# Twelve attention passes on one core: scores computed query by key and transposed after the softmax, against scores computed key by query with row maxima found beforehand

## The chip, the cores and the metric

One core of a Trainium2 chip runs the whole kernel in one launch. The metric is device time in microseconds; the median of three runs counts, and lower is better. PE is TensorE, DVE VectorE, ACT ScalarE, POOL GpSimd; SP issues the loads.

## The reference, cut to what matters

A layer norm, a graph aggregation, a linear attention, and then a block with three chained softmax attentions and an MLP, all on 1250 rows of 512 features. The change concerns the three attentions, each of 8 heads of 64 features: spatial (plain), temporal (causal) and cross, whose queries come from the spatial result and whose keys and values come from the temporal one.

```python
att = softmax(einsum('bthd,bshd->bhts', q, k), axis=-1)      # q scaled by HD ** -0.5
o = einsum('bhts,bshd->bthd', att, v)
spatial_out = _spatial_experts(xn, ...)                      # one expert's weights
temporal_out = _temporal_experts(xt, ...)                    # causal mask, xt + o
fused = _cross_mha(spatial_out, temporal_out, ...)
x = x + fused
```

The result has to be near fp32, so nearly every product is taken in parts: a number is split into a rounded part (`hi`, type fp32r) and the rest (`lo`), and hi x hi, hi x lo and lo x hi are added in PSUM.

## The kernel before, in words

Each engine has its own queue, written out in program order, and they meet by counting semaphores. Attention is 12 passes of two heads each: n = 0 to 3 spatial, 4 to 7 temporal (causal), 8 to 11 cross. The tokens are 10 tiles of 125 rows, two tiles (250) a pair, and a batch is one head of one query pair against one key pair: 50 batches in a full pass, 30 in a causal one, 520 in all.

In a pass PE does, in the order of one list `STEPS`:
- `unit` (L1892): Q and K for both heads, feature by token, in six pieces of 418 columns with 12 matmuls each; ACT writes hi (`unit_hi`, L1124) and DVE lo (`unit_lo`, L1493).
- `values` (L1930): V token by feature, 12 matmuls of 128 columns for each tile, split by ACT (L1163) and DVE (L1549).
- `score` (L1951, L1959, L1961): one query tile against up to 512 keys for the two heads at once, each head in 64 of the array's rows, in three pairs of matmuls; causal pieces add a mask (L1956).
- `turned` (L1976): four transposes of 125x125 of the finished probabilities into PSUM.
- `product` (L1992): four matmuls of 250 columns that add V times the turned probabilities into the one bank `OUT_BANK`.

Between them, DVE takes each score piece out of PSUM scaled, with its row minimum of the negated scores (`shift`, L1516), ACT takes the exponential and its sum over a whole row of up to 1250 keys (`exponent`, L1144), DVE the reciprocal of the sum, one number a row (`recip`, L1529), and POOL multiplies the row by it (`prob`, L940). PE transposes only after POOL. A turned batch is split by ACT (`pt_hi`, L1181) and DVE (`pt_lo`, L1581, which reads PSUM and `pt_hi`). ACT and DVE bring an output out together (L1152, L1539), since the two value parts of a head stand in different halves of the array. Transposes run `AHEAD` = 3 batches ahead of products, in a ring of three banks. The next pass's Q and K stand among the last batches of a pass; passes 0 and 8 have an opening of their own. Before pass 8 the temporal output projection (`project`, L2005) joins in.

POOL splits the weight blocks (`split`, L848 and L850), eight blocks for the folded spatial output projection during pass 1, and the attention outputs in `feat` into planes (`split_plane`, L931 and L933). SP loads 256 KB weight blocks into three slots.

After attention (L2041, L2070) follow the output projection and the MLP, which the change leaves as they are, as it does all before attention.

## Time and profile before

| what | us |
|---|---|
| runs, in order | 2180.33, 2180.38, 2619.19 |
| median | 2180.38 |
| the profiled execution | 2188.32 |
| its span, first to last instruction | 2186.5 |
| mean granted TensorE clock | 0.941 of 2.4 GHz |

The rows below come from the profiled execution. A span starts at its first instruction. Busy time of PE counts overlapping matmuls once, and a matmul's own duration holds its way through the array, so what a matmul costs in a row of like ones is read from start to start. "issue" is time in which an engine waited for nothing that the profile shows.

### The profile page before, as it was taken

To read this page: it belongs to the slowest core of one execution; us is meant where nothing else is said; L and a number is where in the kernel's file an instruction comes from. 1 tells how busy PE (TensorE), PEld (TensorE's weight loads), DVE (VectorE), ACT (ScalarE), POOL (GpSimd) and SP (SyncE) were. 2 spreads that over 40 slices of the span, in tenths; PEclk is the share of its full clock that TensorE was granted. 3 is DMA by queue.
4 is the path that set the end of the run, shared out by engine and by line. 5 is a ranking of instruction groups with operands and counts; after the bars stand their busy time and mean duration, and the time that the engine had idled before them with its cause. 6 is when DMAs were issued, how large, how long until landed. Compare 5 with 4: busy or idle time off the path is not lost.

```text
span 2186.5 us, 35324 instructions
## 1 busy us (share of the span) xinstructions
PE 1885.5 (86%) x11839; PEld 1604.6 (73%) x11839; DVE 1302.4 (60%) x3667; ACT 828.7 (38%) x1490; POOL 602.7 (28%) x575
## 2 busy tenths in 40 slices
PE   1999999866898998989888887888989898876998
PEld 1687577655787886979777776777878786776886
DVE  6576577766676546575645546457676767552332
ACT  0223111022565545565544435246565655320000
POOL 2210011001324315141322213513231315546330
PEclk9999999957999998999989999899999999997999
DMA  3001000023000000020000000000000001002101
GB/s 97 30 6 44 6 25 15 1 104 119 15 1 25 20 30 15 18 92 1 16 1 15 11 6 16 18 6 12 1 16 1 16 1 72 29 28 68 39 29 47
DMA packets 24417, 60.83 MB, mean 28 GB/s; under 512 B 2522, under 2 KB 4790, under 8 KB 23373
## 3 DMA queue, kind: packets, MB, share of 16 engines
q1 hardware_dynamic: 24260, 58.74, 8.0%
q8 instruction: 98, 1.61, 0.3%
q14 instruction: 59, 0.48, 0.1%
HBM read 44.87 MB, written 13.86 MB: 27 GB/s over the span
## 4 chain that ended last, share of the span: by engine, by line
PE 56%; issue 14%; POOL 13%; DVE 10%; ACT 4%; DMA 1%; DVEq 1%; SPq 1%; POOLq 0%; ACTq 0%
PE ps L1892 7%; POOL probs L940 7%; PE ps L1992 7%; PE ps L2041 6%; PE ps L1976 6%; PE ps L1716 5%; PE ps L1930 4%; PE ps L1796 3%; PE ps L2070 3%; PE ps L1828 3%; PE ps L1951 3%; DVE probs L1516 2%; PE ps L1729 1%; DVE pt_lo L1581 1%; ACT pt_hi L1181 1%
## 5 line engine op out<-in xcount | busy, mean ns | idle before, releaser
L940 POOL TENSOR_SCALAR probs<-probs,stats 125x1250 f32<-125x1250 f32 (+4 forms) x240 | 280.8, 1180 | 926.0 <-DVE stats L1529 926.0
L1581 DVE TENSOR_TENSOR pt_lo<-ps,pt_hi 125x500 fp32r<-125x500 f32 x520 | 351.3, 677 | 186.2 <-ACT pt_hi L1181 181.2
L1181 ACT ACTIVATE pt_hi<-ps 125x500 fp32r<-125x500 f32 x520 | 304.8, 588 | 368.0 <-PE ps L1976 363.8
L1976 PE MATMUL ps<-ident,probs 125*125 125x125 f32 x2080 | 332.3, 286 | 87.3 <-POOL probs L940 87.3
L1992 PE MATMUL ps<-pt_hi,v_tok 125*128 125x250 f32 x1040 | 319.0, 328 | 55.5 <-DVE feat L1539 55.3
L1976 PEld LDWEIGHTS ps<-ident,probs 125*125 125x125 f32 x2080 | 285.7, 198 | 103.0 <-POOL probs L940 96.3
L1516 DVE TENSOR_SCALAR_CACHE_REDUCE probs<-ps 125x416 f32<-125x416 f32 (+5 forms) x624 | 340.6, 585 | 16.2 <-PE ps L1961 15.3
L1992 PEld LDWEIGHTS ps<-pt_hi,v_tok 125*128 125x128 f32 x1040 | 204.0, 196 | 139.4 <-DVE pt_lo L1581 77.5
L1144 ACT ACTIVATE probs<-probs,stats 125x1250 f32<-125x1250 f32 (+4 forms) x240 | 286.1, 1193 | 15.1 <-DVE stats L1521 15.1
L1992 PE MATMUL ps<-pt_lo,v_tok 125*128 125x250 f32 x1040 | 274.9, 286 | 0.0
L1992 PEld LDWEIGHTS ps<-pt_lo,v_tok 125*128 125x128 f32 x1040 | 205.5, 198 | 0.4
L1375 DVE TENSOR_SCALAR onehot<-iota_h,win_key,key_t 125x320 f16 x453 | 169.9, 375 | 0.5 <-issue 0.3
L1374 DVE TENSOR_SCALAR onehot<-iota_h,low_t 125x125 f16 x453 | 126.8, 280 | 61.8 <-PE ps L1828 31.8
L1951 PE MATMUL ps<-k_hi,q_hi 64*125 64x416 f32 (+5 forms) x624 | 146.9, 467 | 8.7 <-DVE k_lo L1493 5.8
L1930 PE MATMUL ps<-w_hi,xa_hi 128*125 128x128 f32 x480 | 131.3, 274 | 0.0
L1930 PE MATMUL ps<-w_lo,xa_hi 128*125 128x128 f32 x480 | 130.9, 273 | 0.0
L1930 PE MATMUL ps<-w_hi,xa_lo 128*125 128x128 f32 x480 | 130.8, 272 | 0.0
L1959 PE MATMUL ps<-k_hi,q_lo 64*125 64x416 f32 (+5 forms) x624 | 118.4, 375 | 0.0
L1961 PE MATMUL ps<-k_lo,q_hi 64*125 64x416 f32 (+5 forms) x624 | 114.7, 363 | 0.0
L1828 PE MATMUL ps<-onehot 125*125 x453 | 86.8, 312 | 17.8 <-DVE onehot L1375 17.3
L1796 PE MATMUL ps<-near_rows,adj 125*125 125x257 f32 (+1 forms) x400 | 94.5, 388 | 2.4 <-issue 2.1
L1951 PEld LDWEIGHTS ps<-k_hi,q_hi 64*125 64x125 f32 x624 | 59.8, 188 | 49.4 <-DVE k_lo L1493 7.6
(341 smaller groups left out, 3494.8 us busy)
## 6 DMA issues: line engine op xcount, KB each, us to landing
w_raw<-in_w_mlp SPq DMA_DIRECT2D x32, 256.0 KB, 2.6
w_raw<-in_w_gps SPq DMA_DIRECT2D x16, 256.0 KB, 2.6
w_raw<-in_w_tp SPq DMA_DIRECT2D x16, 256.0 KB, 2.6
w_raw<-in_w_sp SPq DMA_DIRECT2D x12, 256.0 KB, 5.4
w_raw<-in_w_cr SPq DMA_DIRECT2D x12, 256.0 KB, 2.6
d_xt<-xb_hi SPq DMA_DIRECT2D x1, 2508.0 KB, 9.3
d_xt<-xb_lo SPq DMA_DIRECT2D x1, 2508.0 KB, 14.9
xa_hi<-d_xt SPq DMA_DIRECT2D x1, 2508.0 KB, 9.6
```

The source lines that it names most:

```text
L940: pool.tensor_scalar(p, p, stats[:, slot, 7:8], 1.0, ALU.mult, ALU.mult).then_inc(s_prob, 1)
L1144: act.activation(p, p, ACT.Exp, scale=-1.0, bias=st[:, least:least + 1], accum_out=st[:, 4:5]).then_inc(s_exp, 1)
L1181: act.activation(pt_hi[:, (BASE_B[n] + m) % PT, :], ps[0:TOK, ring_bank(ring_of(n, m)), 0:4 * TOK], ACT.Copy)\
L1375: ins = dve.tensor_scalar(row[:, ET:ET + DH], iota_h[0:ET, :], win_key[0:ET, bass.ds(w, 1)], key, ALU.add, ALU.is_equal)
L1516: dve.tensor_scalar(probs[:, slot + h, first:first + w], ps[0:TOK, bank + h, 0:w], -SCALE, None, ALU.mult, ALU.min, accum_out=stats[:, slo ...
L1581: dve.tensor_tensor(pt_lo[:, slot, :], ps[0:TOK, ring_bank(ring_of(n, m)), 0:4 * TOK], f32(pt_hi[:, slot, :]), ALU.subtract).then_inc(s_pt ...
L1796: ins = pe.matmul(ps[0:TOK, bank + h, 0:257 - h], adj[t // 4][:, x, cols], near_rows[:, x, h, 0:257 - h], start=(x == 0), stop=(x == NT - 1))
L1892: ins = pe.matmul(ps[:, x % 4, 0:NP], w[:, k % 3, 128 * c:128 * c + 128], src[:, c, NP * p:NP * p + NP], start=(c == 0 and y == 0), stop=( ...
L1930: ins = pe.matmul(ps[0:TOK, ring_bank(r), 128 * t:128 * t + 128], x[:, c, (t0 + t) * TOK:(t0 + t + 1) * TOK], w[:, k % 3, 128 * c:128 * c ...
L1951: pe.matmul(ps[0:TOK, bank + h, 0:w], q_hi[r, tile], k_hi[r, first:first + w], start=True, stop=False)
L1976: ins = pe.transpose(ps[0:TOK, ring_bank(r), x * TOK:(x + 1) * TOK], probs[:, slot, kt * TOK:(kt + 1) * TOK], ident[0:TOK, 0:TOK])
L1992: ins = pe.matmul(ps[:, OUT_BANK, 0:2 * TOK], v_tok[:, kt, y % 2, :], part[:, slot, 2 * TOK * x:2 * TOK * (x + 1)], start=(kt == 0 and par ...
```

## The change

The attention passes are written anew; what comes before and after stays.

- Scores are computed key by query: 125 keys on the partitions, 250 queries in the columns. The exponential then has the layout that the product with V needs, and the transposes of the probabilities go away, as does POOL's scaling.
- A row maximum can't be taken over partitions, so it is found beforehand: `maximum` multiplies the rounded parts alone, query by key, for both heads at once (L2126), DVE reduces the two banks (L1654), joins the pieces (L1662), PE turns the column of maxima into a row (L2142), and ACT writes it negated into a 65th row of the queries' second operand (L1235), against a row of ones in the keys' operand. The score matmul so subtracts it by itself.
- K and Q are stored twice: `k_both`, `q_both`, `k_rest`, `q_row` hold hi and lo of a head in the two halves of 128 partitions. A score is two matmuls for a key tile: hi keys on 64 rows and again on 64 (against hi and lo queries), then the rest of the keys with the maximum (L2170, L2174). The causal mask is added to the score (L2172).
- ACT takes the exponential of a step's 125x500 scores twice from the same bank: once rounded into `p_hi` and once in full into `p_raw`. DVE subtracts, both inputs in SBUF, into `p_lo`.
- The product has V beside 64 columns of ones (`v_ones`), so the sum of the probabilities stands in the lower half of the output bank, and adds V's rest (`v_rest`) in a matmul of its own: six matmuls for a step. Two banks take turns.
- The end of a unit (one head of one query pair): DVE takes the reciprocal of 64x250 sums, and multiplies (L1686, L1688).
- V is computed feature by token in three pieces, written to `feat` by ACT, and turned by PE (L2152).
- A planner (`plan_steps`) puts the linear pieces K, V, Q, the maxima M, the rows R, the turned values T and the fold F as side tasks between the steps of the pass before, by due dates and costs, and `pool_plan` puts the weight splits 12 steps ahead. Scores run `LEAD` = 2 steps ahead of products; scores and probabilities have rings of three.
- The last plane before the join is split by ACT and DVE, not by POOL.

```diff
+            def exponent(g):
+                act.wait_ge(s_score, g + 1)
+                if g >= PR:
+                    act.wait_ge(s_p_lo, g - PR + 1)
+                if g >= PR:
+                    act.wait_ge(s_pv, g - PR + 1)
+                act.activation(p_hi[:, g % PR, :], ps[0:TOK, g % 3, 0:4 * TOK], ACT.Exp, scale=SCALE).then_inc(s_p_hi, 1)
+                act.activation(p_raw[:, g % PR, :], ps[0:TOK, g % 3, 0:4 * TOK], ACT.Exp, scale=SCALE).then_inc(s_exp, 1)
...
+            def maximum(n, i, y, j):
...
+                dve.wait_ge(s_max, MAX_NO["M", n, i, y, j])
+                dve.tensor_reduce(part[:, y, :, j], ps[0:TOK, 5:7, 0:w], AX.X, ALU.max).then_inc(s_max_part, 1)
...
+            def p_low(g):
+                dve.wait_ge(s_p_hi, g + 1)
+                dve.wait_ge(s_exp, g + 1)
+                if g >= PR:
+                    dve.wait_ge(s_pv, g - PR + 1)
+                dve.tensor_tensor(p_lo[:, g % PR, :], p_raw[:, g % PR, :], f32(p_hi[:, g % PR, :]), ALU.subtract).then_inc(s_p_lo, 1)
+
+            def unit_out(g):
+                n, i, h, _ = STEP[g]
+                u = unit_of(g)
+                dve.wait_ge(s_pv, g + 1)
+                dve.reciprocal(share[:, u % 2, :], ps[64:128, 3 + u % 2, 0:2 * TOK]).then_inc(s_share, 1)
+                dve.wait_ge(s_share, u + 1)
+                dve.tensor_tensor(feat[HALF[h], n % 4, 2 * TOK * i:2 * TOK * (i + 1)], ps[0:64, 3 + u % 2, 0:2 * TOK], share[:, u % 2, :],
+                                  ALU.mult).then_inc(s_o, 1)
...
+                for g in range(first, end):
+                    for what, *at in SIDE[g]:
+                        if what == "M":
+                            maximum(*at)
+                    if g > first and ends(g - 1):
+                        unit_out(g - 1)
+                    if g + LEAD < end:
+                        p_low(g + LEAD)
...
-            def prob(n, u, h):
...
-                pool.tensor_scalar(p, p, stats[:, slot, 7:8], 1.0, ALU.mult, ALU.mult).then_inc(s_prob, 1)
...
+                for x in range(2):
+                    tile = slice((2 * b + x) * TOK, (2 * b + x + 1) * TOK)
+                    to = ps[0:TOK, g % 3, 2 * TOK * x:2 * TOK * (x + 1)]
+                    pe.matmul(to, k_both[h][:, n % 2, tile], q_both[h][:, ring(n, i), :], start=True, stop=False)
...
+                    ins = pe.matmul(to, k_rest[h][rest, n % 2, tile], q_row[h][rest, ring(n, i), :], start=False, stop=True)
...
-                    ins = pe.transpose(ps[0:TOK, ring_bank(r), x * TOK:(x + 1) * TOK], probs[:, slot, kt * TOK:(kt + 1) * TOK],
...
+                    pe.matmul(ps[:, bank, 0:2 * TOK], v_ones[:, kt, h, :], p_hi[:, g % PR, cols], start=(b == 0 and x == 0), stop=False)
+                    pe.matmul(ps[:, bank, 0:2 * TOK], v_ones[:, kt, h, :], p_lo[:, g % PR, cols], start=False, stop=last)
+                    ins = pe.matmul(ps[0:64, bank, 0:2 * TOK], v_rest[:, kt, h, :], p_hi[:, g % PR, cols], start=False, stop=last,
+                                    skip_group_check=True)
```

DVE's queue in a cross pass of the kernel before, around the end of one head's query pair (`pt_lo` is a batch's rest, `probs,stats` a score piece with its minimum, `feat` the output):

```order
L1516 TENSOR_SCALAR probs,stats<-ps 125x416 x2
L1521 TENSOR_REDUCE stats<-stats 125x2
L1529 RECIPROCAL stats<-stats 125x2
L1581 TENSOR_TENSOR pt_lo<-ps,pt_hi 125x500
L1539 SCALAR_TENSOR_TENSOR feat<-ps,vecs,o_half 64x250
L1581 TENSOR_TENSOR pt_lo<-ps,pt_hi 125x500
L1529 RECIPROCAL stats<-stats 125x1
L1581 TENSOR_TENSOR pt_lo<-ps,pt_hi 125x500
L1529 RECIPROCAL stats<-stats 125x1
```

Two rests stand within two instructions of the output, and every reciprocal is one or two numbers wide.

DVE's queue in a cross pass of the changed kernel, at the end of a unit (`p_lo` is a step's rest, `max_part` a maximum's reduction over two banks, `share` the reciprocal):

```order
L1654 TENSOR_REDUCE max_part<-ps 125x2
L1686 RECIPROCAL share<-ps 64x250
L1688 TENSOR_TENSOR feat<-ps,share 64x250
L1679 TENSOR_TENSOR p_lo<-p_raw,p_hi 125x500
L1654 TENSOR_REDUCE max_part<-ps 125x2
L1679 TENSOR_TENSOR p_lo<-p_raw,p_hi 125x500
L1654 TENSOR_REDUCE max_part<-ps 125x2
L1679 TENSOR_TENSOR p_lo<-p_raw,p_hi 125x500
L1654 TENSOR_REDUCE max_part<-ps 125x2
L1662 TENSOR_REDUCE max_col<-max_part 125x2x2
L1679 TENSOR_TENSOR p_lo<-p_raw,p_hi 125x500 x2
```

A reciprocal of one or two numbers a row has become one of 250, with the multiplication behind it, and it stands in front of the next step's rest and the next maximum.

PE's queue in a cross pass before, a batch's transposes, a score piece and a product:

```order
L1976 MATMUL ps<-ident,probs 125x125 x4
L1951 MATMUL ps<-k_hi,q_hi 125x418 x2
L1959 MATMUL ps<-k_hi,q_lo 125x418 x2
L1961 MATMUL ps<-k_lo,q_hi 125x418 x2
L1992 MATMUL ps<-pt_hi,v_tok 128x250
L1992 MATMUL ps<-pt_lo,v_tok 128x250
L1992 MATMUL ps<-pt_hi,v_tok 128x250
L1992 MATMUL ps<-pt_lo,v_tok 128x250
```

Each group works on another batch: the transposes three batches ahead of the product.

PE's queue in a cross pass after, a step's scores, a maximum's pair and a product:

```order
L2170 MATMUL ps<-q_both_a,k_both_a 125x250
L2174 MATMUL ps<-q_row_a,k_rest_a 125x250
L2170 MATMUL ps<-q_both_a,k_both_a 125x250
L2174 MATMUL ps<-q_row_a,k_rest_a 125x250
L2126 MATMUL ps<-k_both_a,q_both_a 125x418
L2126 MATMUL ps<-k_both_b,q_both_b 125x418
L2188 MATMUL ps<-p_hi,v_ones 128x250
L2189 MATMUL ps<-p_lo,v_ones 128x250
L2190 MATMUL ps<-p_hi,v_rest 64x250
L2188 MATMUL ps<-p_hi,v_ones 128x250
L2189 MATMUL ps<-p_lo,v_ones 128x250
L2190 MATMUL ps<-p_hi,v_rest 64x250
```

The four transposes and two of three score pairs are gone; four score matmuls of 250 columns and two more product matmuls have come.

## Rows read from the trace of the kernel before

**Rows 1.** The page, part 1: busy time of the engines.
```profile
PE 1885.5 (86%) x11839; PEld 1604.6 (73%) x11839; DVE 1302.4 (60%) x3667; ACT 828.7 (38%) x1490; POOL 602.7 (28%) x575
```

**Rows 2.** The line that writes outputs: duration ns min/median/max, first and last start us.
```profile
L1539 DVE SCALAR_TENSOR_TENSOR feat<-ps,sp_vecs,o_half x40: 457/476/487, 569.7 to 1040.5; 64x250 f32<-64x250 f32 x40
L1539 DVE SCALAR_TENSOR_TENSOR feat<-ps,tp_vecs,o_half x40: 459/477/489, 1051.7 to 1385.6; 64x250 f32<-64x250 f32 x40
L1539 DVE SCALAR_TENSOR_TENSOR feat<-ps,vecs,o_half x40: 459/475/485, 1471.2 to 1882.0; 64x250 f32<-64x250 f32 x40
```

**Rows 3.** Busy time by stretch: causal, full, all attention.
```profile
core 0: us, PE busy (x) PEld busy (x) DVE busy (x) ACT busy (x) POOL busy (x), PEclk, DMA share, GB/s
1100.00:1200.00 100.00, 82.22 (x599) 72.08 (x597) 53.55 (x151) 47.24 (x101) 24.58 (x29) 0.91 0.03 9
...
1500.00:1600.00 100.00, 93.76 (x711) 81.78 (x709) 69.90 (x201) 58.49 (x103) 25.64 (x21) 1.00 0.02 7
...
515.00:1885.00 1370.00, 1210.30 (x8725) 1054.87 (x8726) 845.68 (x2335) 701.17 (x1276) 436.63 (x417) 0.95 0.06 21
```

**Rows 4.** Waits in attention: us in total, times, longest us.
```profile
PE ps L1976 <- POOL probs L940: 87.3, 39, 5.1
...
PE ps L1992 <- DVE feat L1539: 55.3, 72, 1.6
```

**Rows 5.** PE's timeline in pass 0: start us, us, engine, line, operation.
```profile
641.64 0.38 PE L1992 MATMUL ps<-pt_hi,v_tok 125*128 125x250 f32 x1
641.87 0.28 PE L1992 MATMUL ps<-pt_lo,v_tok 125*128 125x250 f32 x1
641.98 0.28 PE L1992 MATMUL ps<-pt_hi,v_tok 125*128 125x250 f32 x1
...
642.21 0.60 PE L1976 MATMUL ps<-ident,probs 125*125 125x125 f32 x4
642.74 0.45 PE L1951 MATMUL ps<-k_hi,q_hi 64*125 64x418 f32 x2
643.03 0.35 PE L1959 MATMUL ps<-k_hi,q_lo 64*125 64x418 f32 x2
643.22 0.36 PE L1961 MATMUL ps<-k_lo,q_hi 64*125 64x418 f32 x2
643.51 0.38 PE L1992 MATMUL ps<-pt_hi,v_tok 125*128 125x250 f32 x1
```

**Rows 6.** The chain that ended last: start us, us, what.
```profile
515.36 16.30 PE ps L1892 x72
...
624.40 2.30 PE ps L1892 x12
...
785.46 5.39 PE ps L1930 x48
```

**Rows 7.** ACT's groups: operation, shapes, count, busy us, mean ns.
```profile
L1181 ACT ACTIVATE pt_hi<-ps 125x500 fp32r<-125x500 f32 x520 | 304.8, 588 | 368.0 <-PE ps L1976 363.8
...
L1124 ACT ACTIVATE k_hi<-ps,vecs 128x418 fp32r<-128x418 f32 x12 | 7.3, 611 | 21.5 <-PE ps L1892 21.5
```

**Rows 8.** DVE's timeline in pass 0.
```profile
641.38 0.68 DVE L1581 TENSOR_TENSOR pt_lo<-ps,pt_hi 125x500 fp32r<-125x500 f32 x1
641.98 0.58 DVE L1516 TENSOR_SCALAR_CACHE_REDUCE probs<-ps 125x416 f32<-125x416 f32 x1
```

**Rows 9.** Timeline ahead of attention: POOL and DVE, both inputs in SBUF.
```profile
496.43 1.57 POOL L850 TENSOR_TENSOR w_lo<-w_raw,w_hi 128x512 fp32r<-128x512 f32 x1
496.80 1.73 DVE L1293 TENSOR_TENSOR xb_lo<-norm_tmp,xb_hi 128x500 fp32r<-128x500 f32 x1
...
504.13 0.67 DVE L1293 TENSOR_TENSOR xb_lo<-norm_tmp,xb_hi 128x500 fp32r<-128x500 f32 x1
```

**Rows 10.** DVE's groups by form, whole kernel.
```profile
L1539 DVE SCALAR_TENSOR_TENSOR feat<-ps,vecs,o_half 64x250 f32<-64x250 f32 x40 | 18.9, 473 | 7.7 <-ACT o_half L1152 7.2
...
L1493 DVE SCALAR_TENSOR_TENSOR k_lo<-ps,vecs,k_hi 128x418 fp32r<-128x418 f32 x12 | 7.8, 653 | 19.7 <-ACT k_hi L1124 19.7
...
L1413 DVE TENSOR_REDUCE key_st<-mix_k 128x1 f32<-128x1250 f32 x4 | 5.8, 1455 | 13.8 <-ACT mix_k L1050 10.6 <-issue 2.1 <-ACT mix_v L1053 1.1
...
L1257 DVE RECIPROCAL ln_r<-ln_r 125x10 f32<-125x10 f32 x3 | 0.6, 216 | 2.2 <-ACT ln_r L1018 2.2
...
L1622 DVE RECIPROCAL end_r<-end_r 125x4 f32<-125x4 f32 x2 | 0.3, 160 | 0.0
```

More of the change, by code:

```diff
@@ new lines, with key_pieces, maxima @@
+LAST = {(n, i): STEP_NO[n, i, 1, blocks_in(n, i) - 1] for n in range(PASSES) for i in range(5)}
+def key_pieces(n, i):
+    width = 2 * TOK * (i + 1) if CAUSAL[n // 4] else NODES
+    count = -(-width // 512)
+    if count == 3:
+        sizes = [416, 418, 416]
+    elif count == 2:
+        sizes = [width // 2 // 2 * 2, width - width // 2 // 2 * 2]
+    else:
+        sizes = [width]
+    return [(sum(sizes[:j]), sizes[j]) for j in range(count)]
+def maxima(n, i):
+    return [("M", n, i, y, j) for y in range(2) for j in range(len(key_pieces(n, i)))]
@@ L1588, in _ @@
+                for task in SIDE[end - 1]:
+                    last_out(task)
+                unit_out(end - 1)
             for p in range(3):
@@ new lines, in linear @@
+            def linear(role, n, x_hi, x_lo, bank, first, width):
+                pe.wait_ge(s_w_split, NO[role, n] + 1)
+                for c in range(FB):
+                    for y, (w, x) in enumerate(((w_hi, x_hi), (w_hi, x_lo), (w_lo, x_hi))):
+                        ins = pe.matmul(ps[:, bank, 0:width], w[:, ROLE_SLOT[role], 128 * c:128 * c + 128], x[:, c, first:first + width],
+                                        start=(c == 0 and y == 0), stop=(c == FB - 1 and y == 2))
+                return ins
```

1159 lines of the change are left out of this document (636 added, 523 removed).

## The prediction

> **What bounds the kernel now.** The page's first part comes first: PE is busy for 86% of the span, DVE for 60%, ACT for 38% [rows 1]. So PE is the engine to follow. The line that writes an attention output is the clock of the stages: spatial outputs appear from 569.7 to 1040.5 us, temporal ones to 1385.6, cross ones from 1471.2 to 1882.0 [rows 2]. With the first projection at 515.4 [rows 6] attention takes 1367 us of 2186.5; all else is left as it is. By stretches, PE is busy 94% at full clock (1.00, 2.4 GHz) in a spatial or cross pass, and 82% at a mean of 0.91 in a causal one: part of that stretch ran at 1.2 GHz, after waits [rows 3]. The chain of waits says for what: POOL's scaled probabilities, 87.3 us, and the output bank, 55.3 us [rows 4]. So a full pass is PE work with few gaps, and a causal pass loses about a fifth.
>
> Starts in PE's timeline give prices that busy time hides, since matmuls overlap. A 250-column matmul follows its like after 0.115 us; four transposes take 0.53; a score piece (three pairs) 0.77; a product of four 0.57 [rows 5]. Twelve 418-column matmuls take 2.30, 48 of 128 columns 5.39 [rows 6]. A full pass is 50 x (0.53 + 0.57) + 30 x 0.77 + 6 x 2.30 + 120 x 0.112 = 105 us. Four cross passes, less the first unit and the last pass's missing linear work, are some 382 us against 410.8 measured: a factor of 1.07 for waiting.
>
> **PE after.** Out go 2080 transposes and the full-precision score pieces. A step (one head, 250 queries, 250 keys) now is four score matmuls and six product matmuls of 250 columns: 10 x 0.115 + 0.05 for changing over = 1.20 us, so 60 in a full pass. The rough maxima are one pair each, 0.36 by the pair's 0.19 plus a change-over: 30 make 10.8. K and V cost 6 x 2.30, Q in five parts 5 x 12 x 0.115 = 6.9, the turned values and maxima some 4.5. Sum 96 instead of 105; causal 72 instead of about 78.
>
> **ACT after.** Two exponentials of 500 columns a step, by the copy's 588 ns [rows 7] 1.18 us, 59 in a pass, and 25 us of evictions, which double since each half of K and Q is written twice (611 ns for 418 columns [rows 7]). Together 84: it is not the bound, and an exponential with a lead of two steps lies beside products. POOL loses 240 scalings and has room. The same weight blocks are loaded twelve steps ahead of their use; the queues' share is 6% in attention [rows 3], so I cost DMAs at nothing.
>
> **DVE after is the new bound.** Successive DVE instructions overlap by 0.08 us: one of 677 ns is followed after 0.60 [rows 8]. Per full pass:
> - 50 rounded rests at 0.60: 30.0. The inputs are now both in SBUF, which takes the same when POOL is quiet [rows 9].
> - 30 maxima over two banks. A reduction of 1250 elements took 1455 ns [rows 10], 1.05 ns an element plus 0.15 us; 836 elements are 1.03, less overlap 0.95: 28.5, and 1.0 for five joins.
> - 10 unit ends. The reciprocal moves from one number a row to 250 numbers a row. Ten numbers took 216 ns, four 160 [rows 10]: 9.3 ns a number, so 216 + 240 x 9.3 = 2.45 us. With the multiplication behind it (0.47 by the output line [rows 10], with its wait 0.50) it is 2.95: 29.5 in a pass.
> - K 3 x 1.22, Q 5 x 0.87 by the eviction line's 653 ns and its narrower form [rows 10], values 1.9: 10.
>
> Sum 99 us, against 96 for PE; a causal pass 75 against 72. Bounds of the reciprocal: at the lower end it runs as the output line does (0.47), which the two small rows speak against, since they differ by 56 ns for six numbers; at the upper end the slope of 9.3. I take the upper.
>
> **Unit by unit.** A planner's table lays side tasks among the steps. A unit of pass 9 (second query pair, first head) has for DVE 5 x 0.60 + 4 x 0.95 + 0.19 + 0.87 + 2.95 = 10.8, and for PE 5 x 1.20 + 4 x 0.36 + 0.35 + 1.38 = 9.2. The next has two maxima, a third of K and a part of Q: 9.9 for DVE, 10.4 for PE. The buffers reach two or three steps, so the larger engine of each unit counts. Over 120 units these larger values add to 424 + 307 + 388 = 1119 us (spatial, temporal, cross); a single unit of one causal step is 3.6 us of DVE where PE needs 1.2.
>
> Waiting comes on top. The unit end waits for PE's last product of the unit; behind it in DVE's order stand the next rest and the next maximum, for which PE's product and PE's next maximum wait in turn. A score waits for the second exponential three steps back, long done. I walked a unit without linear work: DVE starts a maximum at 0, the unit end at 0.95, and gives the next rounded rest at 4.5. PE has its two earlier products and three scores done by 3.8, and its maximum waits for the bank until 5.45. The round closes after 10.45 us where DVE's sum is 9.75: 1.07. Units with K, V or Q fill that gap. I take 1.06: 1119 x 1.06 = 1187.
>
> What else: the first opening (six projections and two Q parts, 17 us, six maxima through DVE, then row, score, exponential, product) 28 us before the first product; its POOL clears lie beside the K projections. The join at pass 8 has 144 matmuls of 0.19, 27 us, 5 before them for plane 6, 7 behind, and the second opening: 67. Last, the port: beside POOL's subtraction of 1.57 us a DVE subtraction with both inputs in SBUF took 1.73 instead of 0.67 [rows 9]. POOL has 73 such subtractions in attention; about a third meet a rest and cost it 0.6 on average: 15 us. Bounds: 0 where none meet, 73 x 1.06 = 77 where all do; I stay near the share of time that DVE is in this line.
>
> The Trainium skill ("GPSIMD Engine Reference", Specifications) says that GpSimd's SBUF interfaces are shared with VectorE and contended by Vector instructions with two SBUF inputs. By it the old rest, with one input in PSUM, was free of POOL and the new one is not; the trace agrees.
>
> **The sum.** 1187 + 28 + 67 + 15 = 1297 us against 1367: 70 less. The profiled execution took 2188.3 (span 2186.5), so 2118; it lies 8 us above the median of 2180.4, so **2110 us**. About 2% is what a measurement of this kernel can tell from no change: below 2137 is faster, above 2224 slower.
>
> **Rivals.**
> 1. The wide reciprocal is cheap (0.47). DVE falls to 79 a pass, PE bounds it: larger values by unit add to some 1034, x 1.05 + 95 = 1181, so about 1995. For it: nothing but the lack of a wide row. 0.13.
> 2. The maxima couple the queues. PE may start one only when DVE has reduced the last, and DVE comes to it behind a unit end; products behind it stand still. With 1.11 for waiting, 1242 + 110 = 1352: 2165. Against it: only in first-head units do four maxima follow each other. 0.10.
> 3. Slower: the gaps at unit ends cost PE its clock. A stretch busy 82% had 0.91 [rows 3]; a PE that waits at all 120 unit ends is near that. PE's 1036 us of work at 0.90 are 1151; each end adds 1.2 us of wait (0.65 to 1.7), 144. No longer hidden behind DVE, this makes 1295 + 110 = 1405, 38 over before: 2218. It decides from a waiting factor of 1.13 (1119 x 1.13 + 110 = 1375). For it: PE busy would be 87%; against: the waits are 1 to 2 us, while before lost clock behind waits of up to 5. 0.25.
>
> The forecast has 0.52, its own range 2065 to 2160. The range of 2015 to 2230 takes in half of rival 1 and most of rival 3. Faster: four fifths of the forecast and rival 1, with rounding 0.51; within 2%: 0.32; slower: the bad half of rival 3 and a rest, 0.17.
>
> **What would show it.** Right: a reciprocal of some 2.4 us, 120 times, near 290 us; DVE busy over 80% in attention, PE busy for less time than before; PE waiting on the rest and on maxima's reductions, none on POOL; stages of about 477 us (to the last spatial output), 326, and 478 to the end. Wrong: a reciprocal under 0.6 us, ACT above DVE in the chain of waits, or a clock below 0.90 over attention.

## The result and the profile after

| | before | after |
|---|---|---|
| time, median of the runs | 2184.39 us | 2412.80 us |
| profiled execution / span | 2188.32 / 2186.5 us | 2407.93 / 2406.1 us |
| attention, 515.4 us to the last output | 1367 us | 1584 us |

The median of before is over four runs here, the profiled one among them; one of the four, at 2619.19 us, was a slow one and is left out of the ratio. The ratio is 1.105 with a 95% interval of 1.101 to 1.108: slower by a tenth, where the forecast was 2110 us and its range ended at 2230. Attention alone is 217 us longer in the profiled executions, of 219.6 between their spans.

The last outputs of the three parts start at 1129.6, 1496.1 and 2098.6 us in the timeline (for before see [rows 2]): 614, 367 and 603 us, where 477, 326 and 478 were forecast.

Page of after, part 1, which answers to [rows 1]:

```profile
PE 2006.4 (83%) x11351; PEld 1711.8 (71%) x11351; DVE 1548.5 (64%) x2752; ACT 976.1 (41%) x1881; POOL 343.7 (14%) x336
```

Busy time by stretch, all attention first, then 100 us of a full spatial pass and 100 us of a causal one; it answers to [rows 3]:

```profile
core 0: us, PE busy (x) PEld busy (x) DVE busy (x) ACT busy (x) POOL busy (x), PEclk, DMA share, GB/s
515.40:2099.00 1583.60, 1326.00 (x8228) 1158.41 (x8226) 1088.51 (x1415) 846.32 (x1663) 176.09 (x179) 0.88 0.05 18
900.00:1000.00 100.00, 86.27 (x484) 74.25 (x484) 64.13 (x86) 47.23 (x96) 0.00 (x0) 0.77 0.00 1
1300.00:1400.00 100.00, 81.15 (x560) 71.70 (x558) 72.29 (x98) 56.90 (x114) 3.76 (x4) 0.95 0.02 6
```

DVE, which was to be the bound, is busy for 1088.5 of 1583.6 us, 69%. PE is busy for 84% at a mean granted clock of 0.88, where before had 1209 of 1367 us (88%) at 0.95. No engine is full. The second row of stretches is the telling one: PE "busy" for 86 of 100 us, but at 0.77: 41 of the 86 us lie in stretches at 1.2 GHz, so that nearly a quarter of that busy time is matmuls drawn out.

Part 4, the chain that ended last, by engine:

```profile
PE 63%; DVE 17%; ACT 9%; issue 6%; POOL 2%; DMA 1%; DVEq 1%; SPq 1%; POOLq 0%; ACTq 0%
```

DVE stands above ACT in it, as the prediction had it, and POOL has 2%; 17% of 2406 us, over 400, is the part of this chain that runs through DVE.

The groups of instructions by line, with count, busy us, mean ns, and the idle time of their engine ahead of them with what ended it:

```profile
L1679 DVE TENSOR_TENSOR p_lo<-p_raw,p_hi 125x500 fp32r<-125x500 f32 x520 | 374.4, 726 | 168.4 <-ACT p_raw L1265 157.0 <-ACT p_hi L1264 5.2 <-issue 1.7
L1654 DVE TENSOR_REDUCE max_part<-ps 125x2 f32<-125x832 f32 (+5 forms) x312 | 319.5, 1024 | 197.4 <-PE ps L2126 155.8 <-PE ps L2132 38.5
L1686 DVE RECIPROCAL share<-ps 64x250 f32<-64x250 f32 x120 | 206.7, 1722 | 23.4 <-PE ps L2190 20.1
L1688 DVE TENSOR_TENSOR feat<-ps,share 64x250 f32<-64x250 f32 x120 | 49.2, 410 | 4.1
L2126 PE MATMUL ps<-k_both_a,q_both_a 64*125 64x416 f32 (+5 forms) x312 | 157.7, 505 | 134.4 <-DVE max_part L1654 91.7 <-ACT q_row_b L1235 21.7 <-issue 11.5
```

The wide reciprocal takes 1.72 us. PE stands idle for 134 us ahead of maximum pairs (L2126), mostly for the reduction of an earlier pair (L1654). The turned values (L2152) use the same banks and wait for reductions too, so that 131 of PE's 258 us of idle time in attention are waits for a reduction:

```profile
PE ps L2126 <- DVE max_part L1654: 91.7, 67, 3.3
PE ps L2152 <- DVE max_part L1654: 39.1, 28, 3.9
```

DVE stands idle for 156 us ahead of reductions, for PE's pairs, and for 157 us ahead of rests, for ACT's exponentials. Each waits for the other.

One such round, in the timeline of after (start us, us, engine, line, operation; lines left out are PE's other products and scores, and ACT):

```profile
652.95 1.02 DVE L1654 TENSOR_REDUCE max_part<-ps 125x2 f32<-125x832 f32 x1
...
653.99 1.72 DVE L1686 RECIPROCAL share<-ps 64x250 f32<-64x250 f32 x1
654.03 0.45 PE L2126 MATMUL ps<-k_both_a,q_both_a 64*125 64x416 f32 x1
...
655.44 0.28 PE L2170 MATMUL ps<-q_both_a,k_both_a 128*125 128x250 f32 x1
655.56 0.28 PE L2174 MATMUL ps<-q_row_a,k_rest_a 65*125 65x250 f32 x1
655.75 0.41 DVE L1688 TENSOR_TENSOR feat<-ps,share 64x250 f32<-64x250 f32 x1
...
656.19 0.68 DVE L1679 TENSOR_TENSOR p_lo<-p_raw,p_hi 125x500 fp32r<-125x500 f32 x1
...
656.79 1.02 DVE L1654 TENSOR_REDUCE max_part<-ps 125x2 f32<-125x832 f32 x1
657.72 0.67 DVE L1679 TENSOR_TENSOR p_lo<-p_raw,p_hi 125x500 fp32r<-125x500 f32 x1
657.86 0.45 PE L2126 MATMUL ps<-k_both_a,q_both_a 64*125 64x418 f32 x1 [2.03 <-DVE max_part L1654]
...
658.85 0.42 PE L2188 MATMUL ps<-p_hi,v_ones 125*128 125x250 f32 x1
659.06 0.42 PE L2189 MATMUL ps<-p_lo,v_ones 125*128 125x250 f32 x1
```

PE makes a maximum pair at 654.03. DVE has just begun a unit's end, 1.72 and 0.41 us, then a rest, and comes to the reduction at 656.79. PE has run out of other work at 655.8 and its next pair starts at 657.86, after 2.03 us idle. DVE was never idle in that time. Then look at the starts behind it: 658.85 to 659.06 is 0.21 us, where 655.44 to 655.56 was 0.12. The trace has the granted clock at 2.4 GHz up to 658.5 us and at 1.2 GHz from there to 661.9: it fell 0.6 us behind the end of the wait. So a wait of 2 us is paid a second time, in the matmuls that follow it.

**An account of PE's time.** The trace lists the stretches at 1.2 GHz: 26 in attention before, 125 us together, and 63 after, 389 us. Half of PE's busy time inside them is put down as what the clock cost. That is an estimate; 250-column matmuls follow each other there after 0.21 us where they take 0.12 outside. What is left of the busy time is work at full speed, and the rest of attention is idle:

| us of attention | length | work at full speed | idle | lost to half clock |
|---|---|---|---|---|
| before | 1367 | 1154 | 158 | 55 |
| after | 1584 | 1151 | 258 | 175 |

PE's work is equal in both; the 217 us are 100 of idle time and 120 of clock, less 3 of work. The same account is used for the experiments below.

### The profile page after: what moved, and what is told of

Its sections match the earlier page's. It is cut to its first block, busy times and chain, and to the rows that moved or that the text cites. A ratio compares the mean times of both kernels' runs of the same rounds, so it can differ in the third digit from the quotient of the medians.

```text
span 2406.1 us, 34128 instructions
## 1 busy us (share of the span) xinstructions
PE 2006.4 (83%) x11351; PEld 1711.8 (71%) x11351; DVE 1548.5 (64%) x2752; ACT 976.1 (41%) x1881; POOL 343.7 (14%) x336
## 4 chain that ended last, share of the span: by engine, by line
PE 63%; DVE 17%; ACT 9%; issue 6%; POOL 2%; DMA 1%; DVEq 1%; SPq 1%; POOLq 0%; ACTq 0%
PE ps L2068 12%; PE ps L2243 6%; DVE max_part L1654 6%; PE ps L2188 5%; PE ps L1882 5%; PE ps L2126 4%; PE ps L2170 3%; PE ps L2174 3%; PE ps L2189 3%; PE ps L2190 3%; PE ps L1962 3%; DVE share L1686 3%; DVE p_lo L1679 3%; PE ps L2272 3%; ACT p_hi L1264 3%
## 5 line engine op out<-in xcount | busy, mean ns | idle before, releaser
L1679 DVE TENSOR_TENSOR p_lo<-p_raw,p_hi 125x500 fp32r<-125x500 f32 x520 | 374.4, 726 | 168.4 <-ACT p_raw L1265 157.0
L1654 DVE TENSOR_REDUCE max_part<-ps 125x2 f32<-125x832 f32 (+5 forms) x312 | 319.5, 1024 | 197.4 <-PE ps L2126 155.8
L1264 ACT ACTIVATE p_hi<-ps 125x500 fp32r<-125x500 f32 x520 | 306.3, 589 | 318.0 <-PE ps L2174 307.3
L2188 PE MATMUL ps<-p_hi,v_ones 125*128 125x250 f32 x1040 | 341.8, 329 | 16.8 <-DVE p_lo L1679 16.5
L2189 PE MATMUL ps<-p_lo,v_ones 125*128 125x250 f32 x1040 | 306.8, 295 | 0.0
L2190 PE MATMUL ps<-p_hi,v_rest 125*64 125x250 f32 x1040 | 306.3, 295 | 0.0
L1265 ACT ACTIVATE p_raw<-ps 125x500 f32<-125x500 f32 x520 | 304.5, 586 | 0.0
L2126 PE MATMUL ps<-k_both_a,q_both_a 64*125 64x416 f32 (+5 forms) x312 | 157.7, 505 | 134.4 <-DVE max_part L1654 91.7
L2188 PEld LDWEIGHTS ps<-p_hi,v_ones 125*128 125x128 f32 x1040 | 212.2, 204 | 68.1 <-issue 35.5
L1686 DVE RECIPROCAL share<-ps 64x250 f32<-64x250 f32 x120 | 206.7, 1722 | 23.4 <-PE ps L2190 20.1
L2189 PEld LDWEIGHTS ps<-p_lo,v_ones 125*128 125x128 f32 x1040 | 216.6, 208 | 0.5
L2126 PEld LDWEIGHTS ps<-k_both_a,q_both_a 64*125 64x125 f32 x312 | 63.1, 202 | 191.8 <-DVE max_part L1654 109.0
L2126 PE MATMUL ps<-k_both_b,q_both_b 64*125 64x416 f32 (+5 forms) x312 | 158.2, 507 | 0.0
L2174 PE MATMUL ps<-q_row_b,k_rest_b 128*125 128x250 f32 x520 | 147.7, 303 | 0.0
```

The source lines that it names most:

```text
L1264: act.activation(p_hi[:, g % PR, :], ps[0:TOK, g % 3, 0:4 * TOK], ACT.Exp, scale=SCALE).then_inc(s_p_hi, 1)
L1265: act.activation(p_raw[:, g % PR, :], ps[0:TOK, g % 3, 0:4 * TOK], ACT.Exp, scale=SCALE).then_inc(s_exp, 1)
L1654: dve.tensor_reduce(part[:, y, :, j], ps[0:TOK, 5:7, 0:w], AX.X, ALU.max).then_inc(s_max_part, 1)
L1679: dve.tensor_tensor(p_lo[:, g % PR, :], p_raw[:, g % PR, :], f32(p_hi[:, g % PR, :]), ALU.subtract).then_inc(s_p_lo, 1)
L1686: dve.reciprocal(share[:, u % 2, :], ps[64:128, 3 + u % 2, 0:2 * TOK]).then_inc(s_share, 1)
L2126: ins = pe.matmul(ps[0:TOK, 5 + h, 0:w], q_both[h][r, ring(n, i), tile], k_both[h][r, n % 2, first:first + w], start=True, stop=True)
```

## The experiments

Each is an edit of the kernel after, and all ratios are to the kernel before, timed beside it; after itself is at 1.105 (1.101 to 1.108). My forecast's working is theory 1 (DVE's unit ends bound the unit); theory 2 is that PE and DVE wait for each other over the banks of the maxima; theory 3 that PE's own work for them was priced too low; theories 4 to 7 are named where they arise, and so is the load theory, by which the sum of DVE's work counts wherever it stands.

### e1: the reciprocal made cheap

```diff
-dve.reciprocal(share[:, u % 2, :], ps[64:128, 3 + u % 2, 0:2 * TOK])
+dve.tensor_scalar(share[:, u % 2, :], ps[64:128, 3 + u % 2, 0:2 * TOK], 1e-6, None, ALU.mult)
```

> Each unit's end takes a multiply by 1e-6 of its 64x250 row sums in place of their reciprocal, so the division is left out. The reciprocal was 120 x 1.72 us = 207 us of DVE; the multiply should be about 0.35 us. Theory 1 (unit ends on DVE hold up the rests that PE waits for): most of 120 x 1.4 = 165 us comes back, 2240 to 2290 us. Theory 2 (the loss lies in the maxima, in PE's hand-overs through banks 5 and 6): DVE has air anyway (69% busy), so 0 to 60 us come back, 2350 to 2410 us, and PE's waits for max_part stay near 200 us. Clock theory (whatever shortens waits also raises the granted clock): the gain is about twice the waits that go.

Measured: 2324.41 us, ratio 1.062 (1.059 to 1.066), 88 us less than after. The output is no longer right, since the division is left out. The replacement took 0.42 us, so 156 us of DVE's time went, and little over half of it came back. In the profiled executions attention is 73 us shorter: idle fell by 53 us and the clock's loss by 21. Both theories missed: the gain lies between them. DVE's load matters to PE although DVE is idle for a third of the time, but cheap unit ends still leave the kernel 6% slower than before.

### e2: short reductions

```diff
-dve.tensor_reduce(part[:, y, :, j], ps[0:TOK, 5:7, 0:w], AX.X, ALU.max)
+dve.tensor_reduce(part[:, y, :, j], ps[0:TOK, 5:7, 0:32], AX.X, ALU.max)
```

The exponent's scale is 1000 times smaller in e2 and e3, so that nothing overflows; the instructions are the same.

> DVE reduces only the first 32 columns of each piece of scores (the maximum over the others is left out; the exponent's scale is 1000 times smaller so that nothing overflows); PE still makes all 312 pairs. The 320 us of reductions become about 80. Theory 2 (hand-overs of banks 5 and 6): PE's waits for max_part (200 us as PE and PEld) nearly vanish and 100 to 160 us come back, 2250 to 2310 us. Theory 1 (unit ends): the longest DVE jobs stay, so at most 60 us, 2350 to 2400 us. Theory 3 (PE's own work for the maxima is the price, my 0.36 us a pair was too small): 0 to 30 us, about 2390 us.

Measured: 2259.98 us, ratio 1.033 (1.029 to 1.037), 153 us less. From the page of e2 and its waits:

```profile
L1654 DVE TENSOR_REDUCE max_part<-ps 125x2 f32<-125x64 f32 x312 | 69.6, 223 | 204.5 <-PE ps L2126 154.2
```
```profile
PE ps L2126 <- DVE max_part L1654: 35.7, 46, 2.5
```

The reductions fell from 1.02 to 0.22 us. PE's wait for them fell from 91.7 to 35.7 us, its idle time from 258 to 177 and the clock's loss from 175 to 106; its work stayed at 1156. That is theory 2's number: a maximum costs PE through its reduction. It doesn't settle theory 2 alone, since e2 also takes 250 us of work from DVE's queue, and e1 gave back about as much for each microsecond taken. DVE still waits 154 us for the pairs, in a kernel 153 us faster.

### e3: no maxima

```diff
-            tasks += [("Q", n, i)] + maxima(n, i) + [("R", n, i)]
+            tasks += [("Q", n, i)]
...
-                    pe.wait_ge(s_max_in, 5 * n + i + 1)
+                    pe.wait_ge(s_clear, 5)
```

The maxima of the two openings go too, and the 65th row of the queries holds zeros.

> No row maxima at all: the 312 pairs, their reductions, the 60 turned rows and their copies are gone, the row of the queries holds zeros (the subtraction of the maximum is left out; exponent's scale 1000 times smaller). Theory 3 (PE's work alone): 312 x 0.58 + 60 x 0.5 = 210 us, 2200 us. Theory 2 (their waits and the clock that these cost as well): 210 + 100 to 160, 2040 to 2100 us, granted clock over attention up from 0.88 to 0.93 or more. By theory 1 the waits at unit ends stay, so 2200 us or a little below.

Measured: 2013.20 us, ratio 0.921 (0.918 to 0.924), 400 us less, below what every theory had. All of attention in the trace of e3:

```profile
515.40:1705.50 1190.10, 1034.00 (x7326) 987.69 (x7324) 775.41 (x1043) 795.82 (x1543) 178.88 (x175) 0.95 0.07 23
```

By the account: work 981 (170 less than after), idle 156 (101 less), clock 53 (122 less). So this is the whole price of having the maxima beforehand: less than half of it is PE's own work, the rest waiting and clock. What is left, turned scores with the wide reciprocal and both exponentials, beats the kernel before by 8%; it is no kernel to be used, since nothing guards the exponential.

### e4: POOL's copy in place of the second exponential

```diff
-                act.activation(p_hi[:, g % PR, :], ps[0:TOK, g % 3, 0:4 * TOK], ACT.Exp, scale=SCALE).then_inc(s_p_hi, 1)
...
+                pool.tensor_copy(p_hi[:, g % PR, :], p_raw[:, g % PR, :]).then_inc(s_p_hi, 1)
```

> The second exponential goes; POOL copies p_raw to the rounded part as in the sibling (520 copies). ACT loses 520 x 0.59 = 306 us of its 849. Theory 4 (ACT's two exponentials in a row, 1.18 us a step, are what PE waits for through the rests): 30 to 120 us faster, 2290 to 2380 us. My reading (ACT at 53% is not the bound; the copy on POOL takes longer than ACT's and shares DVE's port, so rests stretch from 0.73 to about 1.0 us): 0 to 100 us slower, 2410 to 2510 us.

Measured: 2402.42 us, ratio 1.097 (1.093 to 1.102): the same as after within the intervals. 520 copies of 0.67 us on POOL replace 520 exponentials of 0.59 us on ACT, and rests go from 726 to 735 ns. So theory 4 falls: ACT's load is not what sets the time. How long the way from a score to its rest may be is another matter, since a copy of 0.67 us in place of an exponential of 0.59 leaves that way as long as it was; e10 and e11 ask for that.

### e5: turned values and rows out of the banks earlier

```diff
+                    for task in SIDE[g]:
+                        if task[0] in "RT":
+                            first_out(task)
                     if g + LEAD < end:
                         exponent(g + LEAD)
```

These tasks leave the place behind the exponentials, and the same was done on DVE with `value_lo` ahead of `p_low`.

> Only ACT's and DVE's order changes: the turned values and the turned row of maxima are taken out of banks 5 and 6 ahead of the two exponentials and the rest of the step, no longer behind them, so that PE's next maximum pair finds its banks free earlier. Theory 2 (hand-overs of banks 5 and 6): half of PE's 200 us of waits for max_part (as PE and PEld) come from the 132 turned tasks; 40 to 100 us faster, 2310 to 2370 us. If the wait is DVE's load or PE's own work: within 15 us of 2413 us.

Measured: 2442.39 us, ratio 1.119 (1.115 to 1.123), 30 us slower; a miss of theory 2's number and of the other. The waits of after and of e5:

```profile
ACT v_ones L1247 <- PE ps L2152: 64.8, 34, 7.2
```
```profile
ACT v_ones L1247 <- PE ps L2156: 186.3, 60, 8.6
```

ACT now waits for PE's turned values with the exponentials queued behind, and PE's wait for the reductions is unchanged (91.7 and 94.2 us). What PE waited for was not that turned values and rows left the shared banks late.

### e6: maxima over the full array

```diff
-                pe.wait_ge(s_q_hi, 5 * n + i + 1)
+                pe.wait_ge(s_q_lo, 5 * n + i + 1)
...
-                    ins = pe.matmul(ps[0:TOK, 5 + h, 0:w], q_both[h][r, ring(n, i), tile], k_both[h][r, n % 2, first:first + w],
+                    ins = pe.matmul(ps[0:TOK, 5 + h, 0:w], q_both[h][:, ring(n, i), tile], k_both[h][:, n % 2, first:first + w],
```

The causal mask is added over the full array as well, and since a pair now needs the queries' rest, the planner makes Q one step earlier.

> Each maximum pair as two matmuls over all 128 rows one after the other (rounded queries plus their rest, against the rounded keys) in place of two half arrays side by side; one more step between query and maximum. Of streaming alone a pair of 416 columns costs 0.35 us in place of 0.17 us. If the 0.59 us of a pair is mostly change-over between the half-array and the full-array form (what the timeline of after suggests: 0.21 us before and 0.38 us behind): PE saves 0.1 to 0.2 us a pair, 30 to 60 us in all, and as much again through the waits, 2330 to 2390 us. If the pair's price is streaming and the semaphore: 0.17 us dearer a pair, 50 to 100 us slower, 2460 to 2510 us.

Measured: 2411.30 us, ratio 1.1045 (1.101 to 1.108): no change, a miss of both. What a pair costs is read from starts. After, with half arrays:

```profile
797.05 0.28 PE L2174 MATMUL ps<-q_row_a,k_rest_a 65*125 65x250 f32 x1
...
797.26 0.45 PE L2126 MATMUL ps<-k_both_a,q_both_a 64*125 64x418 f32 x1
...
797.64 0.39 PE L2188 MATMUL ps<-p_hi,v_ones 125*128 125x250 f32 x1
...
797.86 0.28 PE L2189 MATMUL ps<-p_lo,v_ones 125*128 125x250 f32 x1
```

And e6, full arrays one after the other:

```profile
799.81 0.45 PE L2126 MATMUL ps<-k_both_a,q_both_a 128*125 128x418 f32 x1 [0.65 <-DVE max_part L1654]
800.10 0.35 PE L2126 MATMUL ps<-k_both_b,q_both_b 128*125 128x418 f32 x1
800.29 0.28 PE L2187 MATMUL ps<-p_hi,v_ones 125*128 125x250 f32 x1
800.40 0.27 PE L2188 MATMUL ps<-p_lo,v_ones 125*128 125x250 f32 x1
```

With half arrays the row from 797.05 to 797.86 is 0.81 us with two 0.115 us matmuls in it, so the pair costs 0.58. The median of 78 such places at full clock is 0.58 as well. Full arrays take 0.48 to the next product here, and that follows at its usual distance; the medians of 59 and 21 such places, counted in the same way, are 0.45 and 0.39. The Trainium skill ("TensorEngine Tiling (Array Packing)", Key Properties) says that a change of tiling mode drains the engine; the extra 0.1 us on each side in the first piece agrees with it. The account gives 5 us less work, 40 more idle and 34 less clock loss, sum nil. So what a pair saves did not reach the time; the idle time rose where the wait for DVE is, and the account is too coarse to follow the saving further.

### e7: matmuls without use ahead of the waits

```diff
+                if what in ("M", "T", "R") and last_p[0] and STEP[last_p[0]][3]:
+                    bank = 3 + unit_of(last_p[0] - 1) % 2
+                    for _ in range(2):
+                        pe.matmul(ps[0:TOK, bank, 256:384], identb[0:TOK, 0:TOK], identb[0:TOK, 0:128], start=False, stop=False,
+                                  skip_group_check=True)
```

> Two matmuls of 128 columns without use (bf16, into free columns of the bank of the running product) stand ahead of each maximum, turned value and turned row inside a unit, so that PE is active while it would wait there; 0.11 us a time at full clock, some 330 times = 36 us of work, no wait of any other engine changes. Clock theory (short idle stretches cost PE its granted clock, some 120 us more than before): clock over attention up from 0.88 to 0.92 or more, and the time 0 to 60 us below after, 2350 to 2410 us, in spite of the added work. If the clock falls for another reason than PE's idle time: 0 to 40 us slower, 2415 to 2450 us, at the same clock.

Measured: 2404.60 us, ratio 1.100 (1.096 to 1.104), not to be told from after. PE did 45 us more work, its idle time fell by 21 us and the clock's loss by 19. The added work was nearly paid for by these two, but the clock rose only from 0.88 to 0.89 over attention, where the clock theory had 0.92. How much of the 120 us of clock would go if PE were kept busy, and the waits left, stays open.

### e8: the unit's end last in DVE's step

```diff
-                    if g > first and ends(g - 1):
-                        unit_out(g - 1)
                     if g + LEAD < end:
                         p_low(g + LEAD)
+                    if g > first and ends(g - 1):
+                        unit_out(g - 1)
```

> Only DVE's order changes: a unit's reciprocal and multiply stand behind the rest of the step, no longer ahead of it. Theory 1 (the 2.1 us of a unit's end hold up the rest that PE's product needs): 20 to 60 us faster, 2350 to 2390 us. If what DVE's unit ends cost (the 88 us that the cheap reciprocal gave back) is their share of DVE's load between the maxima: within 15 us of 2413 us.

Measured: 2463.86 us, ratio 1.128 (1.124 to 1.131), 51 us slower, a miss of both. DVE's wait for p_raw rose from 157 to 220 us: where it stood, the unit's end filled time in which DVE would have waited for the newest exponentials; behind them it adds to the way to the next reduction.

### e9: each pair handed over head by head

e6's edit, PE's wait for each of the two banks by itself, and on DVE:

```diff
-                dve.wait_ge(s_max, MAX_NO["M", n, i, y, j])
-                dve.tensor_reduce(part[:, y, :, j], ps[0:TOK, 5:7, 0:w], AX.X, ALU.max).then_inc(s_max_part, 1)
+                for h in range(2):
+                    dve.wait_ge(s_max, 2 * MAX_NO["M", n, i, y, j] - 1 + h)
+                    dve.tensor_reduce(part[:, y, h:h + 1, j], ps[0:TOK, 5 + h, 0:w], AX.X, ALU.max).then_inc(s_max_part, 1)
```

> e6_full_array with each pair handed over head by head: DVE reduces the first head's bank while PE still makes the second's, and PE's next maximum waits for each bank by itself (624 reductions of half the size in place of 312, about 0.55 us each, 20 us more DVE in all). If the hand-over of a whole pair (PE 0.35 + semaphore + DVE 1.02 us before either bank is free) is what PE waits for (225 us of waits for max_part in e6_full_array as PE and PEld): waits fall by a third and the time by 30 to 60 us against e6's 2411, 2350 to 2380 us. If DVE is late at the reductions because of what stands ahead of them in its queue: 0 to 20 us slower, 2410 to 2435 us.

Measured: 2400.53 us, ratio 1.098 (1.094 to 1.102), 11 us below e6 with intervals that overlap, and between the two expectations. A finer hand-over is worth about half a per cent, if anything.

### e10 and e11: a ring of four, a lead of three

e10 sets `PR = 4` and lays `p_lo` over `p_raw`. e11 adds `LEAD = 3` and due dates one step earlier.

> Four places for the exponentials in place of three (the rest is written over p_raw, which frees the room), nothing else: an exponential of step g + 2 no longer needs the product of step g - 1, only that of g - 2. If ACT's start behind a product is in PE's way: 20 to 60 us faster, 2350 to 2390 us. My reading: ACT waits mostly for the score (307 us), not for a product, so within 15 us of 2413 us.

> The ring of four and the score issued three steps ahead of its product, not two; the side work's due dates one step earlier. Theory 5 (the chain score, two exponentials, rest, and DVE's other work in its one queue is longer than the two steps of lead, so that small delays on any engine reach PE): the slack of one more step (1.2 us) takes in most of them, idle down by 60 to 120 us and half-clock loss by 30 to 80 us, 2220 to 2320 us. Theory 2 alone (banks 5 and 6 hand over as before whatever the lead): within 25 us of 2413 us, since the maxima still wait for the reduction before.

Measured: e10 2413.33 us, ratio 1.108 (1.103 to 1.112), as expected no change. e11 2464.55 us, ratio 1.130 (1.126 to 1.134): 50 us slower, where theory 5 wanted 90 to 190 less. Theory 2's 25 us are missed too. Slack in the chain of exponentials isn't what is missing. PE's wait for max_part ahead of its pairs is 92.0 us, as in after. Theory 5 falls.

### e12: both

e9's and e11's edits together.

> e9's and e11's edits together. If the two waits are separate, the gains add; if one chain holds both, the sum of e9 and e11 is not reached. By theory 5 and a gain of e9: 2180 to 2290 us, at best the time of the kernel before; by theory 2 alone: as e9, 2350 to 2380 us.

Measured: 2416.30 us, ratio 1.107 (1.104 to 1.111), 48 below e11 and 16 above e9, a miss of both. The longer lead costs less once maxima are handed over by head; neither helps.

### e13 to e16: the order of DVE's queue

By then my theory was that one queue couples the two: the next reduction stands behind a rest whose exponentials hang on the score that PE issues just ahead of the last pair. e13 changes `p_low(g + LEAD)` on DVE to `p_low(g + 1)`; e14 is e11 with `p_low(g + 2)`; e15 is e14 with e9's edits, e16 is e14 with e5's. The clean comparison for e14 is e11, for e15 it is e12.

> Only DVE's order changes: in step g it makes the rest of step g + 1, not of g + 2, so that it no longer waits for the newest exponentials between two reductions. Theory 6 (one queue couples the two: the reduction of the next maximum stands behind a rest whose exponentials hang on the score that PE issues just ahead of the last maximum): DVE's wait for p_raw falls from 157 us to under 60, PE's for max_part from 240 (PE and PEld with the turned tasks) to under 150, and 30 to 100 us come back, 2310 to 2380 us; against it the rest now comes only one step ahead of its product. Load theory (what counts is the sum of DVE's work, as both cheap versions gave time back): within 20 us of 2413 us, or slower by up to 50.

> e11's edits (score and exponentials three steps ahead, ring of four), but the rest two steps ahead, so that its exponentials are a step old when DVE comes to it and the rest is still two steps ahead of its product. Theory 6: better than e13, DVE's wait for p_raw under 30 us, 2250 to 2340 us (e11 was 2465). Load theory: as e11, 2440 to 2480 us.

> e14's edits with e9's (full array, hand-over by head). By theory 6 and e12's gain over e11 (48 us): 2210 to 2300 us. By the load theory: as e12, 2400 to 2440 us.

> e14's edits with e5's (turned tasks out of the banks ahead of the exponentials). e5 lost 30 us because ACT waited for the turned values (186 us) with exponentials due behind them; with a third step of lead that wait should cost nothing and the banks come free earlier: 10 to 40 us below e14. If e5's loss came from elsewhere: above e14.

Measured: e13 2496.93 us, ratio 1.142 (1.136 to 1.147); e14 2437.18, 1.116 (1.110 to 1.122); e15 2393.81, 1.096 (1.091 to 1.100); e16 2476.83, 1.134 (1.130 to 1.139). The waits of e13:

```profile
PE ps L2188 <- DVE p_lo L1679: 125.5, 119, 4.3
...
DVE p_lo L1679 <- ACT p_raw L1265: 37.9, 22, 3.7
PE ps L2126 <- DVE max_part L1654: 34.6, 29, 2.6
```

and of e14:

```profile
PE ps L2127 <- DVE max_part L1655: 79.0, 61, 3.1
...
DVE p_lo L1680 <- ACT p_raw L1266: 33.8, 16, 6.4
```

In e13 both waits fell as theory 6 said (157 to 38, and 92 to 35), and PE's wait for the rest rose from 16.5 to 125.5: the wait moved. In e14 DVE waits 34 us for exponentials in place of 163 in e11, and PE's wait for reductions falls only from 92 to 79. It is 27 us faster than e11, where theory 6 wanted 125 or more, and slower than after. So DVE's wait for exponentials is worth little, and theory 6 falls. e15 is 22 us below e12 and 19 below after, with intervals that just don't meet, but outside both of its expectations. e16 repeats e5: early eviction costs (40 us against e14), also with a longer lead.

### e17 and e18: the maxima spread

```diff
-                due[task] = gf - 6 - (len(tasks) - 1 - x)
+                due[task] = gf - 6 - (len(tasks) - 1 - x) * span // len(tasks)
...
-                if credit < 0.25 and DUE[task] > g + 1:
+                if (credit < 0.25 or task[0] == "M") and DUE[task] > g + 1:
```

Here `span` is the number of steps of the tile before, at most 10. I had first gone through the timeline of after from 560 to 860, 860 to 1130 and 1500 to 1800 us: PE's gaps of over 0.15 us ahead of maximum pairs add to 75 us in these, and DVE was idle in about 12 us of that. PE waits while DVE works, though DVE has air elsewhere.

> Only the planner's dates: a tile's maxima are due spread over the steps of the tile before, and none is taken earlier than a step ahead of its date, so that 125 steps with a maximum follow such a step, not 215, and 35 runs of three steps have one in each, not 155. Theory 7 (in the runs of maxima DVE's work of a step, 1.02 + 0.7 us and a share of the unit end, is as long as PE's, and with one pair of banks each waits for the other there, while in the empty steps DVE idles; its mean of 69% hides that): idle down by 30 to 90 us and with it the half clock, 2270 to 2370 us. Plain load theory or PE's own work: within 20 us of 2413 us.

> e17's dates with e9's full-array pairs handed over by head (e9 gave 13 us). If the small gains add: 2250 to 2350 us. Nothing tried so far removes PE's 187 us for the maxima but leaving them out, so I do not expect the 2180 us of the kernel before.

Measured: e17 2394.59 us, ratio 1.096 (1.094 to 1.099); e18 2391.86, 1.095 (1.092 to 1.098). The waits of e17, which answer to after's 91.7 and 16.5 us:

```profile
PE ps L2127 <- DVE max_part L1655: 56.0, 40, 2.6
...
PE ps L2189 <- DVE p_lo L1680: 36.3, 38, 2.5
```

The spread is worth 18 us, just outside the intervals of both, and far from theory 7's 2270 to 2370. Idle time did not fall (263 us); the wait for reductions went down and those for rests and for the linear parts' banks up. The clock lost 30 us less. Bunching is a small part of the cause, and e18's gains did not add. No version with maxima came near the kernel before; only e3 did better, and it leaves out the subtraction of the maximum.

## Why the prediction was wrong

**What bounds before.** Right: PE with few gaps. Its passes as priced from starts (105 and 78 us) make 1152 us; the account gives 1154 for all of attention.

**PE after.** The step's ten matmuls hold: e3, which is the kernel without maxima, has 981 us of work, and my 1036 + 61 (two openings at 17 us, the join's 27) less my price of the maxima, 312 x 0.36 = 112 and some 18 for their rows, is 967. What was mis-sized is the term "the rough maxima are one pair each, 0.36": a pair of 418 columns costs 0.58 us by the timeline, and all maxima with their rows 170 us by e3, where 130 were taken. In all 1151 us in place of some 1097.

**ACT after.** Right, and e4 shows it: without the second exponential on ACT nothing changes.

**DVE after.** The sum was right by two errors: 8 x 99 + 4 x 75 = 1092 us forecast, 1088.5 measured. The reciprocal is 1.72 us, not 2.45; that is 88 us too much. Other terms were low by about as much: a rest is busy for 726 ns where 0.60 us was taken, 65 us in all, and a reduction for 1.02 where 0.95 was taken, 23 us. The Trainium skill ("VectorE: DVE Perf Modes", First, the fixed hardware budget), from which I estimated 2.2 us, came nearer than the slope of two small rows, but the measurement is below both.

**Unit by unit.** This is the step that failed: "The buffers reach two or three steps, so the larger engine of each unit counts", with 1.06 for waiting. The trace of after can be held against it. With PE's and DVE's queues cut at the unit ends, each unit's PE work at full speed and its DVE busy time add to 1151 and 1093 us, and the larger of the two in each unit (DVE's in 54 of 120) adds to 1214 us, openings and join within it. The forecast's 1119 with 28 for the opening and 67 for the join make 1214 too, in part by luck, since a reciprocal priced too high and a pair priced too low cancel. Attention took 1584: a factor of 1.30 where 1.06 was taken. So this sum was right and the overlap was wrong. The two engines' times don't hide behind each other: PE's queue can't pass a maximum pair whose two banks DVE hasn't reduced, and DVE's queue can't pass a reduction, a rest or a unit's end that waits in turn. The same sum falls by 49 us from after to e1 and by 50 to e2, but attention fell by 73 and by 145. In runs, e1 gives 88 us back for 156 us of DVE's time, e2 153 us for 250: nearly six tenths of each microsecond in both places where it was saved. The prediction walked one unit and found the very wait (PE's maximum until 5.45), then took it as filled by other units. What isn't shown is how much of the 1.30 hangs on there being one pair of banks for the maxima: no run gives them a second pair.

**The clock.** The sum had no term for it beyond what the factor for waiting holds. It lost 55 us before and 175 after, more than the idle time grew (100). e2 and e3 show that it falls back with the waits (to 106 and 53), as the timeline behind 657.86 shows it begin. e7 did not settle how much of it could be held otherwise.

**POOL and DVE's port.** 15 us forecast, added to the time; the rests' longest took 1.76 us against a median of 0.68, and their mean of 726 ns is 520 x 0.048 = 25 us of DVE's time over the median. Small, as said.

**The rivals.** Rival 1 fell by the reciprocal's row. Rivals 2 (the maxima couple the queues) and 3 (gaps cost the clock) both came true, and together: 2165 and 2218 were each taken alone. Their prices over the forecast, 55 + 108, would together have given 2273, still 140 short. What is missing is that not only unit ends make gaps: in the 75 us of gaps counted for e17, DVE was in a reduction for 32 us, in a rest for 16 and in a unit's end for less than 3. I gave the two 0.35 and never their joint case. Of the signs, DVE over 80% and a PE busy for less time than before (1326 us against 1209) did not show; PE waiting on reductions and none on POOL did, and so did one of the signs of being wrong, a clock below 0.90 over attention (0.88).

## What to carry to other kernels

Where two engines hand a buffer back and forth and there is only one of it, their times don't overlap because a mean shows air: price each hand-over as a round (how long until the other engine's queue comes to it, its work, and back) before trusting the larger sum. Here the round was seen for one unit and set aside. Add the granted clock to every sum in which PE gains waits; here it more than doubled the price of the idle time (120 us on 100). Leaving a suspect out entirely (e3) sizes it at once, and should come before any trial of its order.

## What the runs showed of the hardware

- A reciprocal of 250 numbers a row, 64 rows, from PSUM takes 1722 ns; a multiply by a constant of the same shape took 421 ns.
- A pair of 64-row matmuls side by side costs 0.58 us between 128-row ones, for 418 columns, where both as full arrays in turn cost 0.48 in the place shown and 0.39 to 0.45 at the medians (after and e6).
- PE's clock fell to 1.2 GHz behind waits of 1 to 3 us: 49 of the 62 stretches at 1.2 GHz that began in attention of after have a wait of 1.0 to 3.3 us just before them. The kernels with full-array maxima lost less to the clock at more idle time (e6: 141 us lost at 297 idle; after: 175 at 258), which these runs don't explain.
